# Split weights in two buffers and in eighths, split x in DRAM, and the loops written out, in an attention kernel with experts behind it

## The chip, the cores and the metric

The kernel runs on one core of a Trainium2 chip. The metric is the device time of one execution in microseconds (us). Engines are named as in the profile: PE is TensorE (PEld its weight loads), ACT is ScalarE, DVE is VectorE, POOL is GpSimd, SP is SyncE, which only issues DMAs here.

## What is computed

Two layers with residuals on x of shape 8 x 128 x 512, all in f32:

```
q, k, v = x Wq', x Wk', x Wv'          32 query heads, 8 key heads, 128 wide
q, k = rope(rmsnorm(q)), rope(rmsnorm(k))
keys, values = 512 cached rows (gathered by page) + the 128 new ones
p = softmax(mask(q keys' / sqrt(128)))  per query head, 128 x 640
x = x + (p values) Wo'
x = x + x W' + 2 * sum over the top 2 of 8 experts of gate * (x A') B'
```

To keep f32 accuracy on PE every matrix operand is split in two parts of a shorter format, hi (a copy on ACT) and lo (full minus hi, on DVE; for the values on POOL), and each product is three matmuls: hi hi, hi lo, lo hi (`three_passes`, lines 284 to 286).

## The kernel before

The work of the first layer is 64 groups: a group g is key head g // 8 for batch g % 8, with its four query heads. A step s works on several groups at once, in an order that is written out by hand and the same on every engine: scores, softmax and the turned probabilities of group s; the output and the Wo product of group s - 1; norm, rope and turned queries and keys of group s + 1; the projections Q and KV of group s + 2. Steps run from -2 to 64. Steps -2 to 7 are written out, steps 8 to 55 are a loop of six passes over a body of eight steps (`Fori(B, G - B, B)`, i = 8, 16, ..., 48), and steps 56 to 64 are written out again. In the code `step(i, b)` is step i + b. Each engine runs its own copy of this program, and semaphores join them.

PE's order within a step: scores 0 and 1 (L1067), the output O of the group before (L284 to L286), scores 2, turned probabilities T0 (L1091), Q, scores 3, T1, Y (the Wo product), T2, turned queries QT (L1153), turned cached keys KTC (L1075), KV, turned new keys KTN (L1164), T3, and TN (L1170), which is the last of the step. Scores 0 of the next step wait for qt_lo, kt_lo of the cached keys and kt_lo of the new keys. ACT's order: KV copy (L528), square (L533), exp and norm of heads 0 and 1 (L484, L490), o_hi (L557), T0 (L495), v_hi (L571, L572), exp and norm 2, Q copy (L580), T1, exp and norm 3, T2, qt_hi (L602), kt_hi of the cached keys (L500), kt_hi of the new keys (L611), T3, TN (L617). DVE's order: rowmax 0 and 1 (L732), recip 0 (L739), sum of squares (L775), recip 1, o_lo, rowmax 2, u (L811), recip 2, m2 (L818), rowmax 3, pt_lo 0 and 1, recip 3, y (L846), pt_lo 2, qt_lo, kt_lo, kt_lo of the new keys, pt_lo 3 and TN. All hi/lo subtractions on DVE have the line of the helper `low`, L674. POOL does meansq, rstd and wr (L388, L390, L393), rope (L400, L407), v_lo (L413, L414) and issues the gathers (L378).

One buffer holds the split weights of a key head (w_hi, w_lo and, for Wo, wo_hi, wo_lo), and one the raw ones (w_raw, wo_raw). The weights of the next head are split in six pieces of 128 x 512 in steps 5 and 6 of each eight (`query_weights`, and `split_w` for the key and value columns), as soon as the buffer is free, and those of Wo in four such pieces in steps 0 and 1 (`output_weights`, L518 to L523, `split_wo`). PE waits for them in the same steps (`weights_split`, `output_weights_split`). The split x of all eight batches (xt_hi, xt_lo) stays in SBUF from the start on; for the second layer it is overwritten by turned results (`turn_x`) in the last head's steps 6 and 7.

SP loads the whole weights of a head at once:

```
def next_weights(h):
    sp.wait_ge(d_wlo, h * SPLITS)
    sp.dma_start(w_raw[:], wqkv[h]).then_inc(s_wraw, 16)
    sp.wait_ge(d_wolo, h * 4)
    sp.dma_start(wo_raw[:], wo[h]).then_inc(s_woraw, 16)
```

Of the kernel before, what the change touches and what calls it, by code (L numbers as in the profile page):

```python
# [17 lines left out]
B = 8  # L36
# [57 lines left out]

TURN_X = {(6, "Q"): 0, (6, "KV"): 1, (7, "Q"): 2, (7, "QT"): 3, (7, "KTC"): 4, (7, "KTN"): 5, (7, "KV"): 6}


def attention_lora(nc, xT, x, wqkv, wo, kv, normw, kpos, consts, ints, w1, wB, out):
    with ExitStack() as ctx:
# [75 lines left out]
        s_wraw, s_woraw = sem("wqkv_landed"), sem("wo_landed")  # L175
# [22 lines left out]
        d_mark, p_mark = sem("d_mark"), sem("p_mark")  # L198
# [9 lines left out]
        def has(i, off):  # L208

            return not isinstance(i, int) or 0 <= i + off < G  # L210

        def wait(eng, s, i, off, per=1, nth=None):

            add = off * per + (per if nth is None else nth)
            if isinstance(i, int):
                if i + off >= 0:
                    eng.wait_ge(s, i * per + add)
            else:
                eng.wait_ge(s, (i if per == 1 else i * per) + add)

        def carry(eng, i, mark):


            if not isinstance(i, int):
                eng.sem_inc(mark, 1)

        def wait_kv(eng, i, off):

            eng.wait_ge(s_kv[off % 2], i * 32 + 64 * (off // 2 + 1))
# [9 lines left out]
        def first_keys(i, b):  # L239

            return isinstance(i, int) and i == 0 and b == -1

        def first_steps_x(i, b):

            if not (isinstance(i, int) and i == 0 and -1 <= b <= 3):
                return ()
            return (2, 3) if b < 0 else (b + 4,)

        def turned(i, b, unit):

# [24 lines left out]
        SPLITS = KC + 2
# [39 lines left out]

        hflat = ps[:].rearrange("p h k -> p (h k)")
# [5 lines left out]
        def _(sp):  # L322
# [14 lines left out]
            for half in range(2):  # L337
                sp.wait_ge(d_xlo, (half + 1) * HB)
                sp.dma_start(y[:, half * HB:(half + 1) * HB, :], x[half * HB:(half + 1) * HB].rearrange("b s h -> s b h")
                             ).then_inc(s_y[half], 16)  # L340

            def next_weights(h):

                sp.wait_ge(d_wlo, h * SPLITS)
                sp.dma_start(w_raw[:], wqkv[h]).then_inc(s_wraw, 16)
                sp.wait_ge(d_wolo, h * 4)
                sp.dma_start(wo_raw[:], wo[h]).then_inc(s_woraw, 16)

            with sp.Fori(1, HK) as h:
                next_weights(h)  # L350
            sp.wait_ge(d_wlo, HK * SPLITS)
            sp.dma_start(w_raw[:, 0:KC * WL], w1[:, :]).then_inc(s_wraw, 16)
            sp.wait_ge(d_wolo, HK * 4)
# [923 lines left out]
```

## Time and profile before

| | |
|---|---|
| runs | 1254.86, 1263.57, 1258.66 us; median 1258.66 |
| profiled execution, span | 1259.9 us |
| PE busy | 1179.5 us, 94% |
| PEld busy | 1036.0 us, 82% |
| DVE busy | 942.7 us, 75% |
| ACT busy | 931.4 us, 74% |
| POOL busy | 779.0 us, 62% |
| mean granted TensorE clock | 0.984 of full speed |
| HBM read, written | 61.09 MB, 2.10 MB |

Busy time is what the engine's instructions took, without waits. A granted clock of 1.00 is 2.4 GHz, 0.50 is 1.2 GHz. The idle time before an instruction is put down to the instruction whose semaphore came last; "issue" is idle time for which no such instruction is seen.

### The profile page before, as it was taken

The numbers are of one execution on the slowest core, as the hardware profiler recorded it, in microseconds if no ns is written. First come the engines' busy times: TensorE is split into PE (matmuls) and PEld (weight loads), VectorE is DVE, ScalarE is ACT, GpSimd is POOL, SyncE is SP. The second block draws the span as 40 slices with busy tenths as digits, with TensorE's granted clock in tenths as the row PEclk, the third lists the DMA queues.
The fourth block names the chain that finished last, engine by engine and source line by source line (L and its number), as shares of the span: only waits on it lengthen the run. The fifth ranks groups of instructions, "written<-read, shape, count | busy, mean of one in ns | idle before, by whom it ended". The sixth has DMA issues, their size and how long they took to land.

```text
span 1259.9 us, 21986 instructions
## 1 busy us (share of the span) xinstructions
PE 1179.5 (94%) x6912; PEld 1036.0 (82%) x6912; DVE 942.7 (75%) x1833; ACT 931.4 (74%) x1783; POOL 779.0 (62%) x838
## 2 busy tenths in 40 slices
PE   4899999999899989999899998999989999999998
PEld 3778888887888878888788877888878888888787
DVE  7777878777777786778677786777767787877846
ACT  4777877778778877777677776778767877887741
POOL 5566666666666765676566765666656666667500
PEclk8899999999999999999899999999989999999999
DMA  5113022012011121110211111200201111111001
GB/s 208 51 35 142 26 84 68 19 33 85 26 62 35 34 74 31 64 30 26 86 31 54 34 66 39 68 26 26 85 24 63 35 34 62 32 43 34 18 1 67
DMA packets 19434, 64.90 MB, mean 52 GB/s; under 512 B 4832, under 2 KB 5984, under 8 KB 17120
## 3 DMA queue, kind: packets, MB, share of 16 engines
q0 software_dynamic: 12288, 33.57, 8.9%
q1 hardware_dynamic: 7008, 29.64, 6.5%
q8 instruction: 68, 1.11, 0.4%
q14 instruction: 70, 0.57, 0.2%
HBM read 61.09 MB, written 2.10 MB: 50 GB/s over the span
## 4 chain that ended last, share of the span: by engine, by line
PE 68%; DVE 13%; issue 10%; ACT 7%; DMA 1%; DVEq 0%; POOL 0%; SPq 0%; another core or an unknown queue 0%; ACTq 0%; POOLq 0%
PE ps_s L1067 16%; PE ps_w L284 13%; PE ps_w L285 13%; PE ps_w L286 13%; PE ps_w L1091 7%; DVE pt_lo L674 4%; ACT ps L484 3%; DVE ps L732 2%; PE ps_w L1170 2%; PE ps_s L1046 2%; ACT ps L490 2%; PE ps_w L1075 2%; PE ps_w L1153 2%; DVE w_lo L674 1%; ACT pt_hi L495 1%
## 5 line engine op out<-in xcount | busy, mean ns | idle before, releaser
L378 POOL DMA_INDIRECT kv_raw<-kv,rows x256 | 257.5, 1006 | 110.3 <-issue 62.4
L490 ACT ACTIVATE ps<-ps,recip 128x640 f32<-128x640 f32 x256 | 212.8, 831 | 100.1 <-DVE recip L739 96.0
L484 ACT ACTIVATE ps<-ps,negmax 128x640 f32<-128x640 f32 x256 | 211.8, 827 | 79.4 <-DVE negmax L732 72.2
L674 DVE TENSOR_TENSOR pt_lo<-ps_w,pt_hi 128x512 fp32r<-128x512 f32 x322 | 211.9, 684 | 60.0 <-ACT pt_hi L495 55.6
L732 DVE CUSTOM_DVE_ANT_0 ps<-ps_s,mask 128x640 f32<-128x640 f32 x256 | 206.3, 816 | 29.6 <-PE ps_s L1067 26.7
L284 PE MATMUL ps_w<-w_hi,xt_hi 128*128 128x512 f32 (+1 forms) x512 | 185.0, 361 | 10.5 <-DVE w_lo L674 9.9
L495 ACT ACTIVATE pt_hi<-ps_w 128x512 fp32r<-128x512 f32 x256 | 152.0, 594 | 33.8 <-PE ps_w L1091 31.3
L286 PE MATMUL ps_w<-w_hi,xt_lo 128*128 128x512 f32 (+1 forms) x512 | 174.0, 340 | 0.0
L285 PE MATMUL ps_w<-w_lo,xt_hi 128*128 128x512 f32 (+1 forms) x512 | 173.9, 340 | 0.0
L1091 PE MATMUL ps_w<-cst,ps 128*128 128x128 f32 x1024 | 155.2, 274 | 18.9 <-DVE pt_lo L674 11.8
L400 POOL TENSOR_TENSOR rot<-u,cos 128x640 f32<-128x640 f32 x64 | 101.2, 1582 | 113.0 <-DVE u L811 113.0
L1091 PEld LDWEIGHTS ps_w<-cst,ps 128*128 128x128 f32 x1024 | 123.8, 141 | 35.1 <-issue 15.9
L1067 PE MATMUL ps_s<-kt_hi,qt_hi 128*128 128x320 f32 x512 | 124.0, 324 | 20.0 <-issue 18.0
L407 POOL TENSOR_TENSOR rot<-rot,m 128x320 f32<-128x320 f32 x128 | 110.0, 881 | 52.0 <-DVE m L818 52.0
L284 PE MATMUL ps_w<-pt_hi,v_hi 128*128 128x512 f32 x320 | 127.3, 398 | 0.0
L285 PE MATMUL ps_w<-pt_lo,v_hi 128*128 128x512 f32 x320 | 126.5, 395 | 0.0
L286 PE MATMUL ps_w<-pt_hi,v_lo 128*128 128x512 f32 x320 | 125.8, 393 | 0.0
L818 DVE TENSOR_TENSOR m<-u,sin 128x640 f32<-128x640 f32 x64 | 124.5, 1946 | 0.0
L1067 PEld LDWEIGHTS ps_s<-kt_hi,qt_hi 128*128 128x128 f32 x512 | 90.4, 192 | 39.0 <-issue 27.2
L1067 PE MATMUL ps_s<-kt_hi,qt_lo 128*128 128x320 f32 x512 | 119.2, 315 | 0.0
L1067 PE MATMUL ps_s<-kt_lo,qt_hi 128*128 128x320 f32 x512 | 118.8, 314 | 0.0
L284 PE MATMUL ps_w<-wo_hi,o_hi 128*128 128x512 f32 x256 | 106.3, 415 | 12.0 <-DVE wo_lo L674 12.0
(139 smaller groups left out, 2592.3 us busy)
## 6 DMA issues: line engine op xcount, KB each, us to landing
w_raw<-wqkv SPq DMA_DIRECT2D x7, 1536.0 KB
wo_raw<-wo SPq DMA_DIRECT2D x8, 1024.0 KB
kv_raw<-kv,rows POOLq DMA_INDIRECT x256
y<-x SPq DMA_DIRECT2D x2, 1024.0 KB, 5.3
out<-y SPq DMA_DIRECT2D x8, 256.0 KB, 2.2
w_raw<-wqkv SPq DMA_DIRECT2D x4, 384.0 KB, 6.1
w_raw<-w SPq DMA_DIRECT2D x1, 1296.0 KB
y<-xT SPq DMA_DIRECT2D x2, 512.0 KB, 4.2
```

The lines of the kernel that those rows point to most:

```text
L284: nc.tensor.matmul(out_ap, a_hi, b_hi, start=start and k == 0, stop=False)
L285: nc.tensor.matmul(out_ap, a_hi, b_lo, start=False, stop=False)
L286: last = nc.tensor.matmul(out_ap, a_lo, b_hi, start=False, stop=stop and k == n - 1)
L378: pool.indirect_dma_start(kv_raw[:, b % 2, t, :], None, kv[:, :], bass.IndirectOffsetOnAxis(rows[:, b % B, t:t + 1], 0)).then_inc(s_kv[b % ...
L484: nc.scalar.activation(ps[:, h, :], ps[:, h, :], ACT.Exp, bias=negmax[:, b % 2, h:h + 1], scale=-1.0, accum_out=rowsum[:, b % 2, h:h + 1]) ...
L490: nc.scalar.activation(ps[:, h, :], ps[:, h, :], ACT.Copy, scale=recip[:, b % 2, h:h + 1]).then_inc(a_norm, 1)
L495: nc.scalar.activation(pt_hi[:, 0:CT, h, :], bank(f"T{h}").rearrange("p (t q) -> p t q", t=CT), ACT.Copy).then_inc(a_pt, 1)
L674: return nc.vector.tensor_tensor(out_ap, full, hi.bitcast(F32), ALU.subtract)
L732: nc.vector.tensor_tensor_reduce(out=halves(ps[:, h, :]), in0=ps_s[:, h % 2, :, 0:KH], in1=halves(mask[:, b % B, :]), scale=-SCALE, scalar ...
L818: nc.vector.tensor_tensor(m2[:], u[:], sin[:, g1 % B, :].unsqueeze(1).to_broadcast([P, NH, D]), ALU.mult).then_inc(d_m2, 1)
L1067: last = nc.tensor.matmul(ps_s[:, h % 2, half, 0:KH], a, c[:, half * KH:(half + 1) * KH], start=n == 0, stop=n == 2)
L1091: last = nc.tensor.transpose(bank(f"T{h}")[:, t * S:(t + 1) * S], ps[:, h, t * P:(t + 1) * P], ident)
```

## The change

- The step loops of all engines are written out: `step(s)` for s from -2 to 64, all waits on constants. The marks that the loop body needed go.
- w_hi, w_lo, wo_hi and wo_lo have two sides, one for even and one for odd heads. The weights of the next head are split in eighths (W: 128 x 384, Wo: 128 x 256, W of the second layer: 128 x 324), by `W_AT` and `WO_AT` one of each in a step, where steps 0, 2 and 4 have two of W. ACT makes the hi piece between kt_hi of the cached keys and kt_hi of the new keys, DVE the lo piece in the step after, between recip 1 and o_lo. Raw pieces come through rings of three.
- Only two tiles of split x are in SBUF. Each of the eight is stored to DRAM once after its split (`keep_x`), and from group 8 on SP fetches the tile of group s + 4 in its step s (`fetch_x`).
- At the start the first head's query weights land in wr, u, rot and m2, its Wo in the second half of y, and are split from there, Wo in steps -2 and -1. The second half of the transposed x is loaded in step 0. x is split a tile a step, at the end of steps -1 to 4.
- The weight of the experts' second product is split to wo_hi/wo_lo like a Wo piece, no longer to kt_hi/kt_lo at the end. The turned results for the second layer go to a side of w_hi/w_lo and to the two tiles of x.

The diff, cut:

```diff
+SPLITS = KC + 2
+WP = KC * WW // B
+WP1 = KC * WL // B
+OP = REP * HID // B
+W_AT = {}
+for h in range(1, HK + 1):
+    for j in range(B):
+        W_AT.setdefault((0, 0, 1, 2, 2, 3, 4, 4)[j] if h == 1 else B * h - 11 + j, []).append((h - 1) * B + j)
+WO_AT = {s: [s] for s in range((HK - 1) * B + 2)}
+RING = 3
...
-        xt_hi, xt_lo = sb("xt_hi", [P, KC, B * S], F32R), sb("xt_lo", [P, KC, B * S], F32R)
-        w_raw = sb("w_raw", [P, KC * WW])
-        w_hi, w_lo = sb("w_hi", [P, KC * WW], F32R), sb("w_lo", [P, KC * WW], F32R)
-        wo_raw = sb("wo_raw", [P, REP * HID])
-        wo_hi, wo_lo = sb("wo_hi", [P, REP * HID], F32R), sb("wo_lo", [P, REP * HID], F32R)
+        xt_hi, xt_lo = sb("xt_hi", [P, 2, KC * S], F32R), sb("xt_lo", [P, 2, KC * S], F32R)
+        w_raw = sb("w_raw", [P, RING, WP])
+        w_hi, w_lo = sb("w_hi", [P, 2, KC * WW], F32R), sb("w_lo", [P, 2, KC * WW], F32R)
+        wo_raw = sb("wo_raw", [P, RING, OP])
+        wo_hi, wo_lo = sb("wo_hi", [P, 2, REP * HID], F32R), sb("wo_lo", [P, 2, REP * HID], F32R)
+        xsplit = nc.dram_tensor("xsplit", (B, P, 2, KC * S), F32).ap()
...
+        def final_x(b):
+            if b < 6:
+                return w_hi[:, 1, b * KC * S:(b + 1) * KC * S], w_lo[:, 1, b * KC * S:(b + 1) * KC * S]
+            return xt_hi[:, b % 2, :], xt_lo[:, b % 2, :]
...
+        def first_w(k):
+            return (wr, u, rot, m2)[k][:].rearrange("p h d -> p (h d)")[:, 0:QW]
+        first_wo = y[:, HB:B, :].rearrange("p b h -> p (b h)")
...
         (SP)
+            def keep_x(c):
+                sp.wait_ge(a_xhi, c + 1)
+                sp.wait_ge(d_xlo, c + 1)
+                sp.dma_start(xsplit[c, :, 0, :], xt_hi[:, c % 2, :].bitcast(F32)).then_inc(s_xkept[c % 2], 16)
+                sp.dma_start(xsplit[c, :, 1, :], xt_lo[:, c % 2, :].bitcast(F32)).then_inc(s_xkept[c % 2], 16)
+            def fetch_x(g):
+                sp.wait_ge(pe_kv, g - 1)
...
+                sp.dma_start(xt_hi[:, g % 2, :].bitcast(F32), xsplit[g % B, :, 0, :]).then_inc(s_xback[g % 2], 16)
+                sp.dma_start(xt_lo[:, g % 2, :].bitcast(F32), xsplit[g % B, :, 1, :]).then_inc(s_xback[g % 2], 16)
...
+            def w_load(n):
+                sp.wait_ge(d_wlo, SPLITS + max(0, n - RING + 1))
...
+            def wo_load(n):
+                if n >= RING:
+                    sp.wait_ge(d_wolo, REP + n - RING + 1)
...
             for k in range(KC):
+                sp.dma_start(first_w(k), w0[:, k, 0:QW]).then_inc(s_w0[k], 16)
+            sp.dma_start(first_kv, w0[:, :, QW:WW]).then_inc(s_w0kv, 16)
...
             x_transposed(1, 0, 2, 4)
-            x_transposed(2, 1, 0, 4)
-            sp.dma_start(wo_raw[:], wo[0]).then_inc(s_woraw, 16)
...
-            with sp.Fori(1, HK) as h:
-                next_weights(h)
...
+            sp.dma_start(first_wo, wo[0]).then_inc(s_wo0, 16)
+            keep_x(0)
+            keep_x(1)
+            for s in range(-2, G):
+                for n in W_AT.get(s + 1, ()):
+                    w_load(n)
+                for n in WO_AT.get(s + 1, ()):
+                    wo_load(n)
+                if s == 0:
+                    sp.wait_ge(d_wolo, REP)
+                    x_transposed(2, 1, 0, 4)
+                if 2 <= s + 3 < B:
+                    keep_x(s + 3)
+                if s == 0 or s == HB:
+                    natural_x(s // HB)
+                if B <= s + 4 < G:
+                    fetch_x(s + 4)
...
         (ACT)
+            def w_split(n):
+                h = n // B + 1
+                if n % B == 0:
+                    wait(act, pe_q, B * (h - 1) - 1)
+                elif n % B == 1:
+                    wait(act, pe_kv, B * (h - 1) - 1)
+                act.wait_ge(s_wraw[n % RING], 16 * (n // RING + 1))
+                c = w_piece(n)
+                nc.scalar.activation(w_hi[:, h % 2, c], w_raw[:, n % RING, 0:c.stop - c.start], ACT.Copy).then_inc(a_whi, 1)
...
                     if s != -1:
                         cached_keys()
-                if b == 0:
-                    output_weights(0)
-                if b == B - 3:
-                    query_weights(1)
-                if has(i, g1):
-                    wait(act, pe_ktn, i, g1)
+                for n in W_AT.get(s, ()):
+                    w_split(n)
+                for n in WO_AT.get(s, ()):
+                    wo_split(n)
+                if has(g1):
+                    wait(act, pe_ktn, g1)
                     nc.scalar.activation(kt_hi[:, L:KEYS], bank("KTN")[:, 0:S], ACT.Copy).then_inc(a_ktn, 1)
...
+                if s < 0:
+                    first_wo_split(2 * (s + 2))
+                    first_wo_split(2 * (s + 2) + 1)
+                if 2 <= s + 3 < B:
+                    split_x(s + 3)
...
         (DVE)
                     over_sum(1)
...
+                for n in W_AT.get(s - 1, ()):
+                    w_split(n)
+                for n in WO_AT.get(s - 1, ()):
+                    wo_split(n)
+                if has(s - 1):
+                    wait(dve, a_o, s - 1)
                     low(o_lo[:], bank("O"), o_hi[:]).then_inc(d_olo, 1)
...
         (PE)
-                if has(i, g2):
-                    if isinstance(i, int) and i == 0:
-                        pe.wait_ge(d_xlo, min(g2, B - 1) + 1)
+                if has(g2):
+                    if g2 < B:
+                        pe.wait_ge(d_xlo, g2 + 1)
+                    else:
+                        pe.wait_ge(s_xback[g2 % 2], 32 * ((g2 - B) // 2 + 1))
+                        if g2 % B == 0:
+                            pe.wait_ge(d_wlo, SPLITS + g2)
...
-            for b in range(-2, B):
...
-                step(0, b)
-            with pe.Fori(B, G - B, B) as i:
-                for b in range(B):
-                    step(i, b)
-            for b in range(B + 1):
-                step(G - B, b)
+            for s in range(-2, G + 1):
...
+                step(s)
```

## Rows read from the trace of the kernel before

**Rows 1.** The page, part 1: busy us and share of the span.

```profile
PE 1179.5 (94%) x6912; PEld 1036.0 (82%) x6912; DVE 942.7 (75%) x1833; ACT 931.4 (74%) x1783; POOL 779.0 (62%) x838
```

**Rows 2.** Windows: stretch, us, busy us (instructions) by engine, PEclk, DMA share, GB/s.

```profile
49.61:178.70 129.09, 123.73 (x731) 107.62 (x729) 101.60 (x188) 100.82 (x195) 85.82 (x91) 1.00 0.20 69
1069.58:1210.55 140.97, 134.94 (x805) 117.96 (x804) 107.83 (x208) 113.49 (x217) 84.82 (x92) 1.00 0.10 29
...
sum 1160.94, PE 1108.10 PEld 972.17 DVE 881.57 ACT 898.39 POOL 751.36; mean PE 138.51 PEld 121.52 DVE 110.20 ACT 112.30 POOL 93.92
```

**Rows 3.** Windows of single steps, the same columns.

```profile
1140.46:1157.77 17.31, 17.29 (x107) 15.40 (x105) 12.97 (x25) 13.74 (x27) 11.81 (x13) 1.00 0.11 31
470.03:492.86 22.83, 18.93 (x106) 16.78 (x105) 12.71 (x25) 14.36 (x28) 12.27 (x14) 0.93 0.10 27
581.89:601.91 20.02, 18.17 (x106) 15.26 (x105) 16.97 (x31) 15.52 (x30) 12.95 (x13) 1.00 0.23 78
1069.58:1086.88 17.30, 17.30 (x106) 15.41 (x105) 13.06 (x25) 14.24 (x28) 12.26 (x14) 1.00 0.11 31
1086.88:1105.84 18.96, 17.57 (x106) 15.33 (x105) 15.73 (x29) 15.04 (x30) 12.97 (x14) 1.00 0.14 42
```

**Rows 4.** Waits: who waited for whom, total us, times, longest.

```profile
PE ps_s L1067 <- issue: 18.0, 5, 4.1
```

**Rows 5.** Timeline, plain step: start, duration, instruction, [idle before <- releaser].

```profile
1140.22 0.28 ACT L611 ACTIVATE kt_hi<-ps_w 128x128 fp32r<-128x128 f32 x1 [0.84 <-PE ps_w L1164]
1140.54 0.29 DVE L674 TENSOR_TENSOR kt_lo<-ps_w,kt_hi 128x128 fp32r<-128x128 f32 x1 [0.21 <-ACT kt_hi L611]
1141.08 0.52 PE L1067 MATMUL ps_s<-kt_hi,qt_hi 128*128 128x320 f32 x2
1145.58 1.21 POOL L390 TENSOR_TENSOR rstd<-meansq,mhalf 128x5 f32<-128x5 f32 x1
1146.18 0.17 DVE L739 RECIPROCAL recip<-rowsum 128x1 f32<-128x1 f32 x1 [0.97 <-ACT ps L484]
1146.87 1.26 POOL L393 TENSOR_TENSOR wr<-nw,rstd 128x640 f32<-128x640 f32 x1
1147.57 0.48 PE L284 MATMUL ps_w<-w_hi,xt_hi 128*128 128x512 f32 x1
1147.73 0.69 DVE L674 TENSOR_TENSOR o_lo<-ps_w,o_hi 128x512 fp32r<-128x512 f32 x1 [1.38 <-ACT o_hi L557]
1148.35 0.62 ACT L571 ACTIVATE v_hi<-kv_raw 128x512 fp32r<-128x512 f32 x1
1148.87 0.30 ACT L572 ACTIVATE v_hi<-raw 128x128 fp32r<-128x128 f32 x1
1149.08 0.82 DVE L811 TENSOR_TENSOR u<-raw,wr 128x640 f32<-128x640 f32 x1
1154.68 0.69 DVE L846 TENSOR_TENSOR y<-ps_w,y 128x512 f32<-128x512 f32 x1 [0.44 <-PE ps_w L286]
```

**Rows 6.** Timeline, a w_lo split and the POOL operation beside it.

```profile
589.32 1.26 POOL L393 TENSOR_TENSOR wr<-nw,rstd 128x640 f32<-128x640 f32 x1
589.76 1.37 DVE L674 TENSOR_TENSOR w_lo<-w_raw,w_hi 128x512 fp32r<-128x512 f32 x1 [1.42 <-ACT w_hi L439]
```

**Rows 7.** Timeline of the start, the same columns.

```profile
16.81 0.38 ACT L528 ACTIVATE raw<-ps_w 128x256 f32<-128x256 f32 x1 [0.83 <-PE ps_w L286]
18.83 2.86 DVE L693 TENSOR_SCALAR mask<-raw,lenf 128x640 bf16<-128x640 f32 x6
19.52 1.75 POOL L390 TENSOR_TENSOR rstd<-meansq,mhalf 128x5 f32<-128x5 f32 x1
```

**Rows 8.** Windows, DMA queues and issues: the inputs landing, code, transposed x.

```profile
18.00:21.00 3.00, 3.00 (x21) 2.77 (x20) 2.97 (x7) 2.73 (x4) 1.81 (x2) 1.00 0.87 344
q8 instruction: 68, 1.11, 0.4%
y<-xT SPq DMA_DIRECT2D x2, 512.0 KB, 4.2
```

More of the change, by code:

```diff
@@ L197, in attention_lora, with has, wait, wait_kv @@
         d_base, d_gate, d_lg, d_gd, d_hg, d_ht, d_fin = sem("d_base"), sem("d_gate"), sem("d_lg"), sem("d_gd"), sem("d_hg"), sem("d_ht"), sem("d_fin")
-        d_mark, p_mark = sem("d_mark"), sem("p_mark")
         p_init, p_ms, p_rstd, p_wr, p_m1, p_rot = sem("p_init"), sem("p_ms"), sem("p_rstd"), sem("p_wr"), sem("p_m1"), sem("p_rot")
         p_v, p_rows = sem("p_v"), sem("p_rows")
[L208 to L229, printed above, removed]
+        def has(g):
+            return 0 <= g < G
+        def wait(eng, s, g, per=1, nth=None):
+            count = g * per + (per if nth is None else nth)
+            if g >= 0:
+                eng.wait_ge(s, count)
+        def wait_kv(eng, g):
+            eng.wait_ge(s_kv[g % 2], 64 * (g // 2 + 1))
         def bank(unit):
@@ L593, in step @@
-                if has(i, b):
+                turn_x(s, "Q")
+                if has(s):
                     probs(1)
@@ L633, in _ @@
             split_x(1)
+            wh = head_weights(0)[0]
             for k in range(KC):
                 act.wait_ge(s_w0[k], 16)
-                split_w(k, k + 1, 0, QW)
-            split_w(0, KC // 2, QW, WW)
-            split_w(KC // 2, KC, QW, WW)
-            for b in range(-2, B):
-                step(0, b)
-            with act.Fori(B, G - B, B) as i:
-                for b in range(B):
-                    step(i, b)
-            for b in range(B + 1):
-                step(G - B, b)
+                nc.scalar.activation(wh[:, k, 0:QW], first_w(k), ACT.Copy).then_inc(a_whi, 1)
+            act.wait_ge(s_w0kv, 16)
+            for k in (0, KC // 2):
+                nc.scalar.activation(wh[:, k:k + KC // 2, QW:WW], first_kv[:, k:k + KC // 2, :], ACT.Copy).then_inc(a_whi, 1)
+            for s in range(-2, G + 1):
+                step(s)
             def second_expert(c):
@@ L835, in step @@
[L835 to L838 removed]
+                turn_x(s, "Q")
+                if has(s):
                     probs(1)
                     over_sum(3)
[L841 to L845 removed]
+                if 0 < s < B and (s - 1) % HB == 0:
+                    dve.wait_ge(s_y[(s - 1) // HB], 16)
@@ L922, in _ @@
             tab(nc.vector.tensor_copy(langf[:], cin[:, I_LANG:I_END]))
-            for b in range(-2, B):
-                step(0, b)
-            with dve.Fori(B, G - B, B) as i:
-                for b in range(B):
-                    step(i, b)
-            for b in range(B + 1):
-                step(G - B, b)
+            for s in range(-2, G + 1):
+                step(s)
             def largest(b):
@@ L1171, in step @@
                     last.then_inc(pe_tn, 1)
[L1173 to L1174 removed]
+            for s in range(-2, G + 1):
+                if s == -1:
                     pe.wait_ge(s_cst, 16)
[L1176 to L1181 removed]
+                step(s)
             second_layer(3)
@@ L1211, in lora @@
                     pe.wait_ge(d_fin, b - 3)
-                three_passes(result_bank(b), [(pt_hi[:, c, j, :], pt_lo[:, c, j, :], kt_hi[:, 0:HID], kt_lo[:, 0:HID])],
+                three_passes(result_bank(b), [(pt_hi[:, c, j, :], pt_lo[:, c, j, :], wo_hi[:, 0, 0:HID], wo_lo[:, 0, 0:HID])],
                              start=b < B - 1).then_inc(pe_out, 1)
```

637 lines of the change are left out of this document (269 added, 368 removed).

## The prediction

> **What bounds the kernel now.** I read the page's busy shares first: TensorE (PE) is busy 94% of the span, DVE 75% and ACT 74% [rows 1]. So a change pays only where it removes PE idle time, and the others cost only where they delay PE. Next I cut the span at the start of the L1170 transposes, the last PE work of each step. Steps 1 to 63 take 1160.94 us [rows 2]. A step with nothing special takes 17.31, in which PE is busy 17.29 [rows 3]: no reordering gets under that, since the change leaves the PE instructions as they are. 63 x 17.31 = 1090.5, so **70.4 us are excess**: 129.09 - 7 x 17.31 = 7.9 in steps 1 to 7, 140.97 - 8 x 17.31 = 2.5 in steps 56 to 63, and the remaining 60.0 in steps 8 to 55, which are the loop [rows 2].
>
> Single steps say what the 60.0 is. The step after a loop's back edge took 22.83 with a mean granted clock of 0.93, against 17.31 at 1.00 [rows 3]: PE waits for "issue", up to 4.1 us [rows 4], and part of the step then runs at the lower of its two clock levels (1.2 GHz). The step with three of the six weight splits takes 20.02, that with the last two Wo splits 18.96 [rows 3]. So every eight steps pay about 5.5 at the back edge and 5 for splits that come in bunches just ahead of the PE work that reads them.
>
> **The change, part by part.** *Loops written out.* The five back edges go, and with them the drop of the clock that follows idle PE. Steps 56 to 63 are already written out and show the plain 17.31 [rows 3]; the register waits and marks of the loop body also go, at no gain where PE is the bound.
>
> *Splits in eighths.* The same elements are split, but per step one 128x384 piece of W and one 128x256 piece of Wo, one step before they are needed or earlier. The waits of PE for w_lo and wo_lo go; next would be the pieces themselves, and they are done a step ahead.
>
> On ACT both pieces stand right before kt_hi of the new keys (L611). This is the place that matters: L611 releases kt_lo on DVE at 1140.54, and scores(0) of the next step follow at 1141.08 [rows 5]. PE has no slack there. ACT idles 0.84 before L611 [rows 5]. A 128x512 copy from SBUF takes 0.62 and a 128x128 one 0.30, thus 0.83 ns an element; the next starts 0.10 before the end (1148.35 to 1148.87) [rows 5]. So 384 elements occupy 0.41 and 256 occupy 0.31, together 0.72, in a gap of 0.84 + 0.10 = 0.94: **hidden, with 0.22 left**. The step 1069.58 to 1086.88 has a 128x512 Wo split (0.52) in this same place and takes 17.30 [rows 3]. If the cover were gone the cost would be 0.72 a step.
>
> On DVE both pieces stand between recip(1) and o_lo. A 128x512 subtraction takes 0.69, a 128x128 one 0.29 [rows 5], so 384 and 256 take 0.56 + 0.42 = 0.98, in the 1.38 that DVE waits for o_hi [rows 5]. Behind them on DVE are o_lo, rowmax(2), u, m2, rowmax(3), pt_lo twice and recip(3); the first idle time is the 0.44 before y [rows 5]. A delay D of o_lo therefore reaches norm(3) on ACT, and what of D exceeds the 0.22 left reaches PE.
>
> *The shared memory path.* The pieces read two SBUF operands, and POOL computes rstd (from 1145.58 for 1.21) and wr (from 1146.87) at the same time [rows 5]. A w_lo that started 0.44 after wr took 1.37, ending 0.55 after wr did [rows 6]: it was blocked. Here w_lo can start at 1146.3 and wo_lo at about 1146.8, 0.05 to 0.1 before wr. In the start six masks ran back to back in 2.86 through rstd, which took 1.75 in place of 1.21 [rows 7]; so DVE work that is queued back to back held the path and POOL waited. I take D = 0: wr then starts at about 1147.2 and ends at 1148.5, before u at 1149.08 [rows 5].
> The Trainium skill (SBUF — State Buffer, "Who interferes with whom") says that whichever of two such instructions issues first holds the port for its whole length and the other fully blocks. Rows 6 agree. By that rule rstd would hold w_lo back until 1146.8 and the two pieces would end at about 1147.75, still the time at which o_lo starts; if wr gets in between them, it is the first rival.
>
> *x kept in DRAM.* From step 4 on SP fetches 2 x 256 KB per step. The fetch for step s+2's projection is issued when the projections of step s are done. Those end at the latest at 1157.77, where the next step's count begins, and Q's product starts at 1147.57 [rows 5], so the data have 2 x 17.31 - 10.2 = 24.4 us; a 512 KB transposed x landed in 4.2 [rows 8]. SP's waits in front (pieces of three steps before) are over by then. Zero, hidden by more than a step of PE work. Weight pieces are issued two steps ahead: zero. The 56 fetches of 0.52 MB are 29 MB more, some 24 GB/s, where 344 were moved at the start [rows 8].
>
> *The start.* The four first Wo splits move to steps -2 and -1, so ACT now waits for Wo before the KV copy that began at 16.81 after 0.83 idle [rows 7]. DMA still moved 344 GB/s from 18 to 21 [rows 8]; Wo was last. The second half of the transposed x (1.05 MB) now comes later, 1.05 MB / 344 GB/s = 3.0 us, so Wo lands near 18 to 18.5. Two splits of 0.52 follow: the copy starts at about 19.6, **+2.8**. Bounds: +0.2 if Wo is there in time (1.04 less the 0.83 idle), +5.3 if it lands at 21 as before. The chain to scores(0) is otherwise the same.
>
> *Steps 0 to 5.* A split of x (0.52 ACT, 0.6 DVE) now ends each of steps 0 to 4, and steps 0, 2 and 4 have two W pieces. DVE's 0.6 shifts the next step's rowmax(0) and with it norm(3), leaving 0.94 - 0.6 = 0.34 for 0.72 or 1.13: 0.4 or 0.8 late. Over the five following steps and 0.2 in step 0 that is **+3.0**; between 1 and 6. It replaces the 7.9 counted above.
>
> *The end.* Steps 62 and 63 keep their transposes of x: 2.5 less the 1.65 of step 57, **+0.9**. The tail loses one ACT and one DVE split that PE did not wait for: zero.
>
> **Sum.** 1259.9 - 70.4 + 2.8 + 3.0 + 0.9 = 1196.2 for an execution like the profiled one; I add 1.0 for small waits in 57 steps with 0.22 to spare: 1197.2. The median of the runs, 1258.66, is 1.2 lower than the profiled span, so I predict **1196**.
>
> **Rivals.** (1) *The splits do delay o_lo.* wr gets the path between w_lo and wo_lo: wo_lo waits for wr's 1.26, o_lo is late by 0.6 to 1.15. Less 0.22, that is 0.4 to 0.9 in each of 57 steps: 23 to 53 us, 1219 to 1249, likeliest 1220. For it: the start order is decided by 0.1 us, and rows 6. Against: the masks of rows 7. The rule of the SBUF page, cited above, allows either order.
>
> (2) *Written-out code stalls too.* Then "issue" waits were no matter of the loop: the 26 us that five back edges cost (5 x about 5.3) come back as fetch waits, 1196 + 26 = 1222. The change would then not do what it says. For it: 16 KB pieces of code arrive all the time (68 on one queue, 1.11 MB [rows 8]), and now beside more DMA traffic. Against: written-out steps at 17.31 [rows 3].
> The Trainium skill (Advanced Engine Details and Errata, "ISA Cache") says that an engine holds two lines of 256 instructions. A step has 106 or 107 matmuls [rows 3], the loop body of eight some 850 beside as many weight loads, so by this rule looping saved no fetching; no row shows the lines themselves.
>
> (3) *Slower: x comes late.* x has two buffers, and buffer reuse makes a cycle over two steps: the fetch, and the 10.2 us from Q's start to the end of the step. With a landing time T a step takes (T + 10.2) / 2. It decides from T = 24.4, and the kernel is more than 1% slower than now from T of about 27 (1.4 us in each of 54 steps); at T = 30 a step takes 20.1, 2.8 more: 1196 + 151 = 1347. Only the 4.2 of rows 8 speaks on T, and clearly against.
>
> **How the numbers follow.** Forecast 0.69 (1189 to 1206, by the bounds of the start and of the early steps), rival 1 0.16 (0.04 of it at its upper end, within 1%), rival 2 0.11, rival 3 0.04. About 1% (12.6 us) is what a measurement here tells from no change. Faster: 0.69 + 0.12 + 0.11 = 0.92; same 0.04; slower 0.04. The range 1189 to 1224 holds the forecast, the likelier half of rival 1 and most of rival 2, some 0.82.
>
> **What would show it.** In the profile after: L1170 to L1170 at 17.3 in steps 8 to 61; granted clock 1.00 from there on; no "issue" wait of PE at scores; ACT still idle 0.1 before kt_hi of the new keys; o_lo still waiting for o_hi (0.4 or more), and wr stretched to about 1.6 rather than wo_lo to 1.5; the KV copy of the start near 19.6. The prediction is wrong if DVE goes from wo_lo to o_lo without a wait (rival 1), if idle time named "issue" stands in many steps (rival 2), or if PE waits for a DMA at Q (rival 3).

## The result: 1195.7 us, and the profile after

The changed kernel took **1195.74 us** (median of 4 runs, 1195.42 to 1196.66), beside 1259.5 for the kernel before on the same chip (4 runs, 1254.86 to 1263.57). The ratio is **0.950, 95% interval 0.947 to 0.954**. The forecast was 1196. The profiled execution has a span of 1193.7 us, where before it was 1259.9; the sums below are made between these two.

The page after, its first part, the granted clock in the 40 slices and the shares of the chain of waits:

```profile
PE 1155.7 (97%) x6912; PEld 1025.5 (86%) x6912; DVE 928.4 (78%) x1880; ACT 938.9 (79%) x1830; POOL 768.2 (64%) x838
...
PEclk9899999999999999999999999999999999999999
...
q8 instruction: 57, 0.93, 0.3%
...
PE 85%; DVE 5%; ACT 5%; issue 3%; DMA 1%; SPq 1%; POOL 0%; DVEq 0%; POOLq 0%; ACTq 0%
```

PE executes as many matmuls as in [rows 1] and is busy in 97% of a shorter span. The written-out program fetched less code, 0.93 MB against the 1.11 of [rows 8].

Windows, cut as in [rows 2, 3] at the start of the last transposes of a step (L1119 now): steps 1 to 7, steps 8 to 55, steps 56 to 63, then step 1, step 2 and step 33 alone. The columns are those of [rows 2].

```profile
51.28:176.67 125.39, 122.58 (x730) 107.40 (x730) 102.99 (x197) 102.34 (x205) 83.94 (x92) 1.00 0.31 102
176.67:1007.63 830.96, 830.14 (x4995) 739.20 (x4994) 658.70 (x1296) 691.25 (x1345) 574.34 (x625) 1.00 0.25 81
1007.63:1145.19 137.56, 133.86 (x806) 117.62 (x804) 105.37 (x209) 111.47 (x215) 83.44 (x92) 1.00 0.16 53
51.28:69.82 18.54, 17.77 (x106) 15.28 (x105) 15.78 (x30) 14.76 (x31) 12.03 (x14) 1.00 0.42 142
69.82:87.47 17.65, 17.39 (x106) 15.30 (x105) 14.15 (x28) 14.70 (x29) 11.91 (x14) 1.00 0.24 78
609.45:626.76 17.31, 17.29 (x107) 15.40 (x106) 13.76 (x27) 14.42 (x29) 11.97 (x13) 1.00 0.25 81
```

The second row is the result: 48 steps in 830.96 us, 48 x 17.31 = 830.9, with PE busy in all but 0.8 of them. These steps had 60.0 us of excess before; now they have none. Step 33, with its two weight pieces, is as long as the plain step of [rows 3], which had none. What is left of the excess stands in the first row (125.39 - 7 x 17.31 = 4.2).

The waits after, of the engines that the prediction named (who waited for whom, total, times, longest):

```profile
DVE o_lo L664 <- ACT o_hi L568: 41.7, 61, 3.2
PEld ps_s L1011 <- issue: 13.4, 57, 0.5
ACT wo_hi L493 <- DMA y<-wo: 5.5, 1, 5.5
```

The waits of 4.1 at the scores [rows 4] are gone, none is over 0.5 on the weight loads. DVE still waits for o_hi in nearly every step, so in those the pieces ended before o_hi did.

The timeline of a normal step (step 33), for comparison with [rows 5]. R, the start of reciprocal 1, is 615.20:

```profile
614.59 1.21 POOL L417 TENSOR_TENSOR rstd<-meansq,mhalf 128x5 f32<-128x5 f32 x1
...
615.20 0.16 DVE L734 RECIPROCAL recip<-rowsum 128x1 f32<-128x1 f32 x1 [0.99 <-ACT ps L527]
615.28 0.54 DVE L664 TENSOR_TENSOR w_lo<-w_raw,w_hi 128x384 fp32r<-128x384 f32 x1
...
615.74 0.42 DVE L664 TENSOR_TENSOR wo_lo<-wo_raw,wo_hi 128x256 fp32r<-128x256 f32 x1
615.87 1.40 POOL L420 TENSOR_TENSOR wr<-nw,rstd 128x640 f32<-128x640 f32 x1
...
616.75 0.69 DVE L664 TENSOR_TENSOR o_lo<-ps_w,o_hi 128x512 fp32r<-128x512 f32 x1 [0.59 <-ACT o_hi L568]
```

The two pieces end at 616.16, 0.59 before o_lo. Two things are to be seen. w_lo starts 0.69 after rstd did, inside it, and takes its plain 0.54: rstd, 1.21 long for 128x5 elements, doesn't hold it up. And wo_lo starts 0.13 before wr; wr is stretched from 1.26 to 1.40 and wo_lo is not stretched.

In the other order rstd does wait. In step 27 it started 0.01 behind w_lo and took 1.60:

```profile
511.37 0.54 DVE L664 TENSOR_TENSOR w_lo<-w_raw,w_hi 128x384 fp32r<-128x384 f32 x1
511.38 1.60 POOL L417 TENSOR_TENSOR rstd<-meansq,mhalf 128x5 f32<-128x5 f32 x1
```

### The profile page after: what moved, and what is told of

Read it like the earlier page. It is cut to its first block, busy times and chain, and to the rows that moved or that the text cites. A ratio compares the mean times of both kernels' runs of the same rounds, so it can differ in the third digit from the quotient of the medians.

```text
span 1193.7 us, 20774 instructions
## 1 busy us (share of the span) xinstructions
PE 1155.7 (97%) x6912; PEld 1025.5 (86%) x6912; DVE 928.4 (78%) x1880; ACT 938.9 (79%) x1830; POOL 768.2 (64%) x838
## 3 DMA queue, kind: packets, MB, share of 16 engines
HBM read 90.45 MB, written 6.29 MB: 81 GB/s over the span
## 4 chain that ended last, share of the span: by engine, by line
PE 85%; DVE 5%; ACT 5%; issue 3%; DMA 1%; SPq 1%; POOL 0%; DVEq 0%; POOLq 0%; ACTq 0%
PE ps_s L1011 18%; PE ps_w L282 16%; PE ps_w L281 16%; PE ps_w L280 16%; PE ps_w L1034 8%; PE ps_w L1119 2%; PE ps_w L1102 2%; PE ps_s L993 2%; PE ps_w L1019 2%; ACT ps L527 2%; DVE pt_lo L664 2%; ACT ps L533 1%; DVE ps L727 1%; DMA y<-wo 1%; ACT pt_hi L538 1%
## 5 line engine op out<-in xcount | busy, mean ns | idle before, releaser
L406 POOL DMA_INDIRECT kv_raw<-kv,rows x256 | 254.0, 992 | 93.8 <-issue 62.7
L280 PE MATMUL ps_w<-pt_hi,v_hi 128*128 128x512 f32 x320 | 124.9, 390 | 0.0
L280 PEld LDWEIGHTS ps_w<-w_hi,xt_hi 128*128 128x128 f32 x512 | 97.2, 190 | 20.8 <-DVE xt_lo L664 8.2
```

The costliest lines, as they stand in the source:

```text
L280: nc.tensor.matmul(out_ap, a_hi, b_hi, start=start and k == 0, stop=False)
L406: pool.indirect_dma_start(kv_raw[:, g % 2, t, :], None, kv[:, :], bass.IndirectOffsetOnAxis(rows[:, g % B, t:t + 1], 0)).then_inc(s_kv[g % ...
```

## The experiments

The runs were made on three chips, on which the kernel before took 1255.66, 1256.79 and 1259.46 us (medians). Its executions lie between 1250.4 and 1263.6; those of a written-out kernel lie within 3 us of each other.

**Which part brings what.** *Loops written out, nothing else*: the kernel before, with the loop of each of the five queues that have one (SP, POOL, ACT, DVE, PE) as a loop of the program that writes the code, so that every step is written out. Two of the five:

```diff
-            with sp.Fori(1, HK) as h:
+            for h in range(1, HK):
...
-            with pe.Fori(B, G - B, B) as i:
+            for i in range(B, G - B, B):
```

> The kernel before with its loops written out and nothing else changed. My theory: the steps after the five back edges (20.50, 22.83, 23.95, 22.08, 23.47 us in the trace of before) become 17.31, which is 26.3 us; two irregular steps inside the loop (10 and 33) may give 3.6 more. The time is 1229 to 1234, and the weight steps keep their 5.2 us in every eight. Rival (written-out code waits for its fetch too): the stalls named issue come back elsewhere, at most 5 us are gained, 1254 or more. The other 33 us or so of the change would then be the splits.

Measured: 1229.23 us (1228.36 to 1229.46, 4 runs), ratio 0.979 (0.976 to 0.982), profiled span 1227.3. Its windows: steps 1 to 7, 8 to 55, 56 to 63, then step 24, which followed a back edge before (the 22.83 of [rows 3]), and step 33, which has weight splits:

```profile
48.62:177.68 129.06, 123.67 (x731) 107.58 (x729) 101.47 (x188) 100.75 (x195) 85.15 (x90) 1.00 0.20 69
177.68:1038.48 860.80, 837.96 (x4995) 738.29 (x4994) 667.09 (x1260) 684.86 (x1309) 579.93 (x625) 1.00 0.16 48
1038.48:1179.04 140.56, 134.57 (x806) 117.46 (x804) 107.70 (x208) 113.22 (x216) 84.25 (x92) 1.00 0.10 29
464.52:481.83 17.31, 17.29 (x107) 15.41 (x106) 12.96 (x25) 14.26 (x28) 11.81 (x14) 1.00 0.12 33
625.23:644.17 18.94, 17.56 (x107) 15.32 (x106) 15.72 (x29) 15.02 (x30) 12.97 (x14) 1.00 0.25 83
```

The five steps that followed a back edge are plain, 17.30 to 17.33 at a clock of 1.00. In steps 8 to 55 the excess fell from 60.0 to 860.80 - 830.9 = 29.9: half of it was the loops, and the other half, which the changed kernel also removes, was the splits in bunches. In spans, 32.6 us of the 66.2 come from the loops (1259.9 to 1227.3) and 33.6 from the rest of the change (1227.3 to 1193.7). The first of these depends on the execution of the kernel before that was profiled; by medians on the chip of this run the loops bring 26.4 (1255.66 to 1229.23).

**How much room is left beside the pieces.** *ACT makes each W piece twice*, the second time into a tile that nobody reads:

```diff
+                if n >= B:
+                    nc.scalar.activation(extra[:, 0:c.stop - c.start], w_raw[:, n % RING, 0:c.stop - c.start], ACT.Copy)
```

> The changed kernel with each W piece from head 2 on copied on ACT once more, into a spare tile, 0.42 us more in the gap ahead of kt_hi of the new keys in 56 steps. My theory: the gap has about 0.22 left (0.12 of it visible idle time), so kt_hi, kt_lo and scores 0 come 0.2 to 0.3 late in each of these steps, no step hides it, and the time is 1196 + 11 to 17 = 1207 to 1213. Rival (PE is bound by its own queue and kt_hi has more slack than that): no change, 1196.

Measured: 1204.19 us (1204.13 to 1204.24), ratio 0.959 (0.956 to 0.963). A step takes 17.49 in place of 17.31: the extra piece occupies 0.41, of which 0.18 reaches PE. So ACT had 0.23 left before kt_hi, as the prediction's 0.94 - 0.72 = 0.22 has it. 48 steps with 0.18 and five with 0.08 (narrower pieces) make 9.0, and the total is 8.5 above the changed kernel's. The mechanism was right, and PE now waits where it should, for kt_lo before scores 0; the expected 11 to 17 was too large.

```profile
194.76 0.53 PE L1014 MATMUL ps_s<-kt_hi,qt_hi 128*128 128x320 f32 x2 [0.20 <-DVE kt_lo L667]
```

*DVE makes each W piece twice*:

```diff
+                if n >= B:
+                    low(extra[:, 0:c.stop - c.start], w_raw[:, n % RING, 0:c.stop - c.start], w_hi[:, h % 2, c])
```

> The changed kernel with each W piece from head 2 on subtracted on DVE once more, into a spare tile, 0.47 us more between recip 1 and o_lo in 56 steps. My theory: DVE still waits 0.59 us for o_hi there and wr starts only later, so it is hidden: 1196, within 2 us. Rival (the path shared with POOL decides): wo_lo now meets wr or rstd, takes about 1.5 in place of 0.42, o_lo is about 0.9 late and PE 0.5 or more in each of 56 steps: 1220 or more.

Measured: 1224.55 us (1223.61 to 1225.48), ratio 0.975 (0.972 to 0.979). **My theory failed and the rival held**: DVE had 0.59 of waiting left and the extra piece is 0.46 long, yet each step takes 17.91, 0.60 more. The timeline of one step, R = 164.78:

```profile
164.78 0.16 DVE L737 RECIPROCAL recip<-rowsum 128x1 f32<-128x1 f32 x1 [0.97 <-ACT ps L528]
164.87 0.54 DVE L665 TENSOR_TENSOR extra<-w_raw,w_hi 128x384 fp32r<-128x384 f32 x1
...
165.32 0.55 DVE L665 TENSOR_TENSOR w_lo<-w_raw,w_hi 128x384 fp32r<-128x384 f32 x1
165.48 1.51 POOL L421 TENSOR_TENSOR wr<-nw,rstd 128x640 f32<-128x640 f32 x1
...
165.79 1.48 DVE L665 TENSOR_TENSOR wo_lo<-wo_raw,wo_hi 128x256 fp32r<-128x256 f32 x1
```

wr was waiting while w_lo ran, and it, not the next DVE piece, went in when w_lo was done: 165.48 + 1.51 = 166.99 is the end of wr, and wo_lo (0.42 alone) ends 0.28 behind it. DVE instructions queued back to back don't keep the path.

o_lo is 0.87 late in these steps, and 0.60 of it reaches PE, but not by the way that the prediction names (ACT's gap before kt_hi). PE doesn't wait for kt_lo at scores 0; it waits for qt_lo before the transposes T3, which go into the PSUM bank that qt_lo reads:

```profile
212.32 0.63 PE L1037 MATMUL ps_w<-cst,ps 128*128 128x128 f32 x4 [0.28 <-DVE qt_lo L665]
```

**Is it the work or the meeting with wr?** *One small copy more on DVE*, 128x128 elements between reciprocal 1 and w_lo in steps 6 to 61:

```diff
+                if 6 <= s <= 61:
+                    nc.vector.tensor_copy(extra[:], ident)
```

> The changed kernel with one small extra VectorE copy (128x128, about 0.2 us) between reciprocal 1 and the weight pieces, in steps 6 to 61 (56 steps). Theory (what decides is whether wo_lo begins before wr does, a margin of 0.13 us): wr gets in first, wo_lo is blocked behind it, o_lo is some 0.65 us late, 0.4 us of it beyond ScalarE's slack: about 0.43 x 56 = 24 us more, 1220. Rival (only VectorE's work counts, and 0.59 us of its wait for the attention output is left): 1196.

Measured: 1195.18 us (1194.94 to 1195.43), ratio 0.949 (0.946 to 0.952), no loss: my number was wrong. The timeline of step 7:

```profile
164.64 0.21 DVE L769 COPY extra<-cst 128x128 f32<-128x128 f32 x1
164.76 0.55 DVE L665 TENSOR_TENSOR w_lo<-w_raw,w_hi 128x384 fp32r<-128x384 f32 x1
165.23 0.42 DVE L665 TENSOR_TENSOR wo_lo<-wo_raw,wo_hi 128x256 fp32r<-128x256 f32 x1
```

```profile
165.23 1.54 POOL L421 TENSOR_TENSOR wr<-nw,rstd 128x640 f32<-128x640 f32 x1
```

The copy moved wo_lo by only 0.13, to the very start of wr, and it still went first; wr took the delay (1.54). The run shows that the order holds down to a tie. It did not reach the point beyond, so it doesn't tell the theory from the rival: the run with the doubled piece and wr held back does, below.

*The same, and wr held back until wo_lo is done*:

```diff
+                    if 6 <= s <= 58:
+                        pool.wait_ge(d_wolo, REP + s)
                     nc.gpsimd.tensor_tensor(wr[:], nw[:], ...)
```

> The run before it, and wr (GpSimd) also waits until VectorE's half of the Wo piece of its step is done (steps 6 to 58). wr then runs at about R+1.2 to R+2.5 (R is the begin of reciprocal 1) and u needs it at R+2.9. Theory (the loss is the meeting of wr and wo_lo, not VectorE's work): 1196 to 1199 (the three steps without that wait may keep 0.4 each). Rival (the work itself is the loss, or a later wr delays u): 1220 or more.

Measured: 1196.47 us (1196.41 to 1196.52), ratio 0.950 (0.947 to 0.953). wr starts 0.59 later (R + 1.26) with its plain 1.26, and steps 8 to 55 take 831.1 as they did (831.0). The 1.3 us more in the total arose before, in step 0, whose last transposes came 1.56 later in the profiled execution and where wr isn't held. Since there was no loss to cure, this shows only that holding wr costs nothing.

*The doubled DVE piece, and wr held back in the same way* (steps 1 to 58):

> The kernel with VectorE's subtraction for each W piece done twice (1224.6 us without the next edit), and wr waits until VectorE's half of the Wo piece of its step is done. Theory: the three subtractions end at about R+1.45, just before o_lo's R+1.54, wr at about R+2.8, just before u's R+2.9: 1196 to 1200. Rival (VectorE's extra work is itself too much, or u waits for wr): 1215 to 1225.

Measured: **1193.86 us** (1193.36 to 1194.36), ratio 0.948 (0.945 to 0.951), where the doubled piece alone had taken 1224.55. One wait on GpSimd takes back 31 us with the same work on DVE (2.5 of it in steps 1, 3 and 5). A step of it, R = 162.99:

```profile
163.07 0.54 DVE L667 TENSOR_TENSOR extra<-w_raw,w_hi 128x384 fp32r<-128x384 f32 x1
163.53 0.55 DVE L667 TENSOR_TENSOR w_lo<-w_raw,w_hi 128x384 fp32r<-128x384 f32 x1
164.00 0.42 DVE L667 TENSOR_TENSOR wo_lo<-wo_raw,wo_hi 128x256 fp32r<-128x256 f32 x1
164.54 0.69 DVE L667 TENSOR_TENSOR o_lo<-ps_w,o_hi 128x512 fp32r<-128x512 f32 x1
```

```profile
164.59 1.26 POOL L423 TENSOR_TENSOR wr<-nw,rstd 128x640 f32<-128x640 f32 x1 [1.00 <-DVE wo_lo L667]
```

wo_lo is 0.42 again, o_lo starts at R + 1.55 as in the changed kernel, and wr beside o_lo (which reads one operand from PSUM) slows neither. This settles that the price was the meeting of wr and wo_lo.

**Where the pieces stand.** *DVE's pieces behind o_lo* in place of before it:

```diff
+                if has(s - 1):
+                    wait(dve, a_o, s - 1)
+                    low(o_lo[:], bank("O"), o_hi[:]).then_inc(d_olo, 1)
                 for n in W_AT.get(s - 1, ()):
                     w_split(n)
                 for n in WO_AT.get(s - 1, ()):
                     wo_split(n)
```

> The changed kernel with VectorE's two halves of each weight piece moved from between reciprocal 1 and o_lo to the place right behind o_lo. wr (GpSimd) and the pieces then don't meet before o_lo, so o_lo starts where it did, but the two pieces (0.43 + 0.54 us undisturbed, up to 0.86 late in all) push rowmax 2, norm 3 and what hangs on them. My theory (no wait of VectorE behind o_lo is free): about 0.6 us more in each of some 57 steps, 1226 to 1240 us. Rival (there is slack behind o_lo too, as there was before it): 1196.

Measured: 1230.17 us (1229.50 to 1230.84), ratio 0.979 (0.974 to 0.984). Steps take 17.86 in place of 17.31. The pieces are undisturbed here (0.55 and 0.42), DVE waits the full 1.38 for o_hi again, rowmax 2 follows 0.80 later, and PE waits 0.28 for qt_lo before T3 as with the doubled piece: the wait before o_lo is worth using, the time behind it is not free.

*The pieces in pairs*, two in every second step, with a ring of four:

```diff
-        W_AT.setdefault((0, 0, 1, 2, 2, 3, 4, 4)[j] if h == 1 else B * h - 11 + j, []).append((h - 1) * B + j)
+        W_AT.setdefault((0, 0, 1, 2, 2, 3, 4, 4)[j] if h == 1 else B * h - 10 + j // 2 * 2, []).append((h - 1) * B + j)
```

> The changed kernel with the W pieces made in pairs, two in every second step instead of one in each: the same work in all, in half the steps. Theory (what a step hides is its own wait: two pieces on VectorE delay o_lo by 0.86 us less the 0.63 us that ScalarE still has free there, and two on ScalarE cost 0.2): 1202 to 1212. Rivals: only the total of work counts, 1196; or each paired step loses as steps 1, 3 and 5 do (1.2 us in each of some 28), 1230.

Measured: 1212.19 us (1211.55 to 1212.84), ratio 0.965 (0.960 to 0.970). Steps with DVE's pair take about 18.15, those between 17.11, together 0.65 above two of 17.31, where 0.4 was worked out; the time lies at the upper end of the range. PE's waits in a pair step show both parts:

```profile
195.30 0.53 PE L1012 MATMUL ps_s<-kt_hi,qt_hi 128*128 128x320 f32 x2 [0.22 <-DVE kt_lo L665]
212.11 0.63 PE L1035 MATMUL ps_w<-cst,ps 128*128 128x128 f32 x4 [0.27 <-DVE qt_lo L665]
```

The first comes from ACT's pair in the step before: 0.2, as expected. The second is that of the doubled DVE piece, with the same 0.87 of delay of o_lo and, as there, some 0.60 lost. The expectation took off 0.63 that ACT has free before kt_hi in this step, and that slack didn't help, since the delay reaches PE earlier, at T3. The step after gives 0.2 back.

**Are the fetches of x hidden?** *No fetches* (the projections of group 8 and later, from step 6 on, read what the two x buffers hold already, so other x data from head 1 on):

```diff
-                if B <= s + 4 < G:
-                    fetch_x(s + 4)
```

> The changed kernel without the fetches of split x and without PE's wait for them; from group 8 on the projections take the two tiles of x that were split last, so this part of the computation uses other data, in the same instructions. My theory: the 56 fetches of 0.52 MB are wholly hidden, so 1196, within 2 us. Rival (DMA traffic slows gathers, code fetch or weights): 3 us or more faster.

Measured: 1196.06 us (1195.57 to 1196.55), ratio 0.953 (0.949 to 0.956), with 61.09 MB read from HBM in place of 90.45. The 29 MB cost nothing.

**The start.** In the changed kernel ACT waits 5.5 us in all for Wo, and the copy of K and V stands behind it:

```profile
19.20 1.15 ACT L493 ACTIVATE wo_hi<-y 128x512 fp32r<-128x512 f32 x2 [5.48 <-DMA y<-wo]
20.25 0.36 ACT L548 ACTIVATE raw<-ps_w 128x256 f32<-128x256 f32 x1
```

*The first four Wo slices split later*: ACT behind the sine tables, DVE two at the end of step -1 and two in step 0:

```diff
 # ACT, step -1, behind the tables          # DVE
+for h in range(REP):                        +if s == -1: first_wo_split(0); first_wo_split(1)
+    first_wo_split(h)                       +if s == 0:  first_wo_split(2); first_wo_split(3)
```

> The changed kernel with its start rearranged: ScalarE makes the four high parts of the first Wo slices behind the sine tables in step -1 in one stretch, VectorE two low parts at the end of step -1 and two in step 0 behind reciprocal 1. Theory (the first Wo pieces, waiting for their transfer, hold up the K/V copy and with it scores 0, 3.4 us later than in the kernel before): 1191 to 1193. Rival (the start is bounded by the transfers and the tables, the order does nothing): 1195 to 1196.

Measured: 1194.36 us (1193.70 to 1195.42, 5 runs), ratio 0.951 (0.947 to 0.954): 1.4 less than the changed kernel, and less than was expected. The copy of K and V began at 16.62, 3.6 earlier, but in step 0 the two wo_lo parts took 2.37 where 1.27 is their own (below), rowmax 2 waited, and PE reached the transposes T2 only 2.4 earlier (45.03 in place of 47.42). Of the 2.4 another 1.0 was lost behind T2, where the clock was lower. The windows from T2 to the last transposes of step 0, here and in the changed kernel:

```profile
45.03:49.89 4.86, 4.86 (x29) 4.86 (x30) 2.59 (x5) 4.07 (x10) 3.98 (x6) 0.66 0.08 16
47.42:51.28 3.86, 3.56 (x30) 3.23 (x30) 2.41 (x5) 3.51 (x10) 3.28 (x5) 1.00 0.00 0
```

PE had waited 3.77 before T2 here and 2.63 there.

*And the first W pieces spread over more steps*, (-1, -1, 0, 1, 2, 3, 4, 4) for (0, 0, 1, 2, 2, 3, 4, 4):

> As the run before it, and the first eight W pieces of head 1 spread over steps -1, -1, 0, 1, 2, 3, 4, 4 in place of steps 0 to 5 with doubled ones. Theory (steps 1, 3 and 5 with two pieces were 18.54 us for want of a place for the second): about 1 us less than the run before it, 1190 to 1192. Rival (the second piece costs the same wherever it stands): the same time as the run before it.

Measured: 1193.32 us (1191.66 to 1194.61), ratio 0.949 (0.946 to 0.953), but with the same profiled span, 1192.2 against 1192.3. Steps 1 and 3 came down from 18.60 and 18.52 to 17.72 and 17.66, and step 0 went up by 1.6: DVE's two W pieces stand in it now, so T2 came 0.9 later behind a wait of 4.35, and the rest of the step took 0.75 more at a clock of 0.56. In the profiled executions the gain was moved, not saved, as the rival has it. The medians are 1.0 apart, as the theory has it, but the five runs of each overlap: this stays open.

*The rearranged start, and wr held until DVE's pieces are done in steps 0, 1, 3 and 5*:

> The rearranged start (1194.4 us), and in steps 0, 1, 3 and 5, which have two pieces of the same kind on VectorE, wr waits until they are done. Theory: steps 1, 3 and 5 come from 18.54 to about 17.66 as their neighbours (2.6 us), and step 0, where wo_lo took 1.78 us beside wr for 0.67, gives up to 1 us: 1190 to 1192. Rival (u then waits for wr and gives it back): 1194 to 1195.

Measured: **1190.81 us** (1190.03 to 1192.09, 5 runs), ratio 0.945 (0.943 to 0.947), the best version. Steps 1, 3 and 5 take 17.7 each in place of 18.5 to 18.6. The last transposes of step 0 came no earlier (49.84 against 49.89):

```profile
37.00 1.27 DVE L665 TENSOR_TENSOR wo_lo<-y,wo_hi 128x512 fp32r<-128x512 f32 x2
38.19 0.82 DVE L728 CUSTOM_DVE_ANT_0 ps<-ps_s,mask 128x640 f32<-128x640 f32 x1
...
39.73 0.83 DVE L787 TENSOR_TENSOR u<-raw,wr 128x640 f32<-128x640 f32 x1 [0.72 <-POOL wr L422]
```

The two parts are down to 1.27 for both, and PE reached T2 2.1 earlier (42.91 against 45.03), though u now waits 0.72 for wr. Behind T2 that was lost again:

```profile
42.91:49.84 6.93, 6.29 (x29) 5.89 (x30) 2.75 (x6) 4.28 (x10) 5.75 (x8) 0.51 0.08 21
44.64 1.12 PE L1106 MATMUL ps_w<-cst,rot 128*128 128x128 f32 x4 [0.64 <-POOL rot L436]
```

The rival's mechanism is the smaller part: u late, so rot late, 0.64 of waiting. The larger is that PE ran this stretch at a clock of 0.51 in place of 0.66. Why it fell further here, after a shorter wait, stays open.

## Why the prediction was right, point by point

**The loops and the bunches (70.4 us of excess).** Right, in size and in cause. From step 7 to step 61 every step takes 17.31, to within 0.04. The loops alone gave back 30.1 us in steps 8 to 55: 26.3 in the five steps behind a back edge, on which the text put about 5.3 each, and 3.6 in steps 10 and 33. Rival 2 (written-out code stalls too) is excluded by the run with the loops alone: none of its steps 1 to 63 has a lower clock, and it fetched 0.92 MB of code in place of 1.11. The Trainium skill (Advanced Engine Details and Errata, "ISA Cache") gives two lines of 256 instructions, but also 128 KB on TensorE where the other engines have 32, and the text used the two lines for PE's matmuls. By that page's figures 128 KB would be 2048 instructions (an estimate), more than the 1700 or so matmuls and weight loads of the loop body, so that looping could have saved fetching on PE. No row shows the lines themselves; the fetched totals went the other way.

**The pieces on ACT.** Right: 0.22 left by the working, 0.23 by the doubled piece, and ACT still idles 0.12 before kt_hi of the new keys (step 20). The add of 1.0 for small waits was not needed; there were none.

**The pieces on DVE.** D = 0 was right, **its second reason was wrong**. The text said that DVE work queued back to back held the path in the start, by the masks and the stretched rstd of [rows 7]. The runs show that wr goes in between two DVE pieces as soon as it waits: in the doubled-piece kernel in nearly every step, in the changed kernel itself in steps 1, 3 and 5. What carries D = 0 is the first reason alone, that wo_lo starts before wr does (0.13 us measured, 0.05 to 0.1 worked out). Rival 1 was thus closer than its chance said, though the margin is steady: it held in all normal steps, and down to a tie in the run with the small copy. The detail "wr stretched to about 1.6" came out as 1.40. A second thing was wrong in the price of rival 1: what of a delay of o_lo reaches PE was right in size (0.87 - 0.22 = 0.65 by the text, 0.60 measured), but its way was not. It goes by norm 3 and then qt_lo to T3, ahead of kt_hi, as PE's waits in the runs with the doubled piece and with the pairs show. The Trainium skill (SBUF — State Buffer, "Who interferes with whom") says that the first to issue holds the port for its whole length. For wr and the pieces the rows agree: wr went first where its record starts first (165.48 against wo_lo's 165.79), wo_lo where its own does. For rstd they don't, if its recorded length is taken as it stands: w_lo started in the middle of it and took 0.54.

**Steps 1 to 5.** The term that was mis-sized in its parts: 2.8 predicted for steps 1 to 5, 4.4 measured there (4.2 over steps 1 to 7), and by another mechanism. The text charged x's splits and ACT's doubled pieces, 0.4 and 0.8 in turn. In fact steps 1, 3 and 5 cost 1.2 each and steps 2 and 4 cost 0.35. In the former DVE has its two W pieces, one step behind ACT's, and rival 1 takes place:

```profile
57.65 1.01 DVE L664 TENSOR_TENSOR w_lo<-w_raw,w_hi 128x384 fp32r<-128x384 f32 x2
...
58.26 1.51 POOL L420 TENSOR_TENSOR wr<-nw,rstd 128x640 f32<-128x640 f32 x1
...
58.58 1.48 DVE L664 TENSOR_TENSOR wo_lo<-wo_raw,wo_hi 128x256 fp32r<-128x256 f32 x1
...
59.98 0.68 DVE L664 TENSOR_TENSOR o_lo<-ps_w,o_hi 128x512 fp32r<-128x512 f32 x1
```

o_lo starts right behind wo_lo, 0.87 late. Holding wr back made these steps 17.7, which proves 0.8 of the 1.2. The 0.35 to 0.4 that is left stands in all five steps; it fits x's splits, behind which DVE's work stands 0.4 to 0.6 later than in the steps after, but no run took them away. ACT's doubled pieces cost next to nothing: they would fall on the step behind, 1, 3 or 5. In steps 3 and 5 PE does wait 0.22 for kt_lo, but with wr held back these steps are within 0.05 of steps 2 and 4 (17.66).

**x in DRAM.** Right: nothing, by the run without fetches. Rival 3 is excluded.

**The start.** The mechanism was right: ACT waits for Wo before the copy of K and V, which began at 20.25 (19.6 predicted, 16.81 in [rows 7]). The term was +2.8. PE reached T2 of step 0 3.3 later (44.09 to 47.42), but the last transposes of the step only 1.7 later (49.61 to 51.28). Most of the difference is the clock: from T2 on it was 0.69 in the profile before and 1.00 in the one after (a further 0.57 was a wait for pt_lo, which is gone). This differs between executions. In eight more kernels with the same start the last transposes came from 50.29 to 52.55; four of them had a clock of 1.00 behind T2 and took 3.84 from there, four had 0.65 to 0.67 and took 4.84 to 4.94. So +1 to +3 is what can be said, and which of the two a run gets stays open.

**The end.** Sign wrong, 0.9 predicted and -0.9 measured in steps 56 to 63. The text charged 17.31 to every step. Step 63 has less PE work (93 matmuls) and is not bound by it: it took 17.38 in the run with the loops alone, which keeps the splits of before, and 15.98 in the changed kernel. The tail came out 0.8 shorter.

**The sum.** Predicted changes to the span: -70.4 + 2.8 + 3.0 + 0.9 + 1.0 = -62.7. Measured: -70.4 + 4.2 (steps 1 to 7) + 0.0 (8 to 55) - 0.9 (56 to 63) + 1.7 (start and step 0) - 0.8 (tail) = -66.2. The span was overestimated by 3.5. That the median was met within 0.3 is partly luck. The text took off 1.2 because the profiled span before lay that far above the median time. But the time of a run is 1.7 to 1.9 above its core's span in every run on record, so that the span after is 2.0 below its median; the text had this offset nowhere. The 1.2 that was taken off and the 2.0 that was left out cover all but 0.3 of the 3.5.

## What to carry to other kernels

When a step is bound by one engine, cut the span at the same instruction of each step, take the shortest step as the floor, and count the excess over it: that sum was good to 4 us in 1260. Work that is put into another engine's wait has to fit in order as well as in length: two SBUF operands on VectorE beside a GpSimd operation cost up to 1.1 us when GpSimd gets in first. Where the GpSimd result is not urgent, one wait that holds it back until VectorE's piece is done costs nothing and removed that loss (1224.6 to 1193.9, and 1194.4 to 1190.8 in the best version).

## What the runs showed of the hardware

- A GpSimd operation that waits for the path gets it at the end of the running VectorE instruction, ahead of the next one in VectorE's queue: wo_lo 1.48 in place of 0.42, wr 1.51 in place of 1.26. At a tie of starts VectorE went first (wr 1.54, wo_lo 0.42).
- rstd (128x5, a power, 1.21 us) didn't block a VectorE subtraction that started 0.69 into it (0.54); wr (128x640, 1.26 us) did. Started 0.01 behind such a subtraction, rstd itself took 1.60.
- A VectorE subtraction with one operand in PSUM (o_lo, 0.69) ran through wr with no loss to either (0.69 and 1.26).
- In the kernel with loops the five steps behind a back edge took 20.50 to 23.95 (22.83 with a clock of 0.93); written out, with nothing else changed, they took 17.30 to 17.33 at 1.00, and the program fetched less code (0.92 MB) than the one with six passes of a loop (1.11 MB).
- After a wait of PE of 2.4 to 2.6 us before T2 in step 0, the rest of the step took 3.84 us at a clock of 1.00 in five profiled executions and 4.84 to 4.94 at 0.65 to 0.67 in four others.
